# A new order of the four engines' queues in the expert feed-forward stages of a macaron block

## The reference

```
sim    = h @ Wq against the keys               # 4 heads, 2 x 64 keys
scores = top 8 of (top 8 of sx + top 8 of sy)  # pairs of keys = experts
w      = silu((h . down_embed) * softmax(scores))
experts = sum over chosen experts of w * up_embed
dense   = silu(h @ W_up.T) @ W_down.T          # 1024 hidden
x = x + 0.5 * (dense + experts)
```

## Time and profile before

| | |
|---|---|
| median of 3 runs | 3957.12 us (3955.64 to 3960.07) |
| profiled execution | 3957.12 us, span 3955.3 us |
| granted TensorE clock, mean | 0.973 |
| PE busy | 3690.7 us, 93% |
| DVE busy | 3255.2 us, 82% |
| ACT busy | 2747.0 us, 69% |
| POOL busy | 2457.3 us, 62% |

### The profile page before, as it was taken

One profiled execution on the slowest core, in us unless ns is written; L12 is line 12 of the kernel. 1 busy time (PEld: TensorE's weight loads), 2 busy tenths in 40 slices (PEclk: granted clock), 3 DMA queues, 4 the chain that ended last, 5 costly groups with the idle time before them and its releaser, 6 DMA issues. The chain is left out here.

```text
span 3955.3 us, 79090 instructions
## 1 busy us (share of the span) xinstructions
PE 3690.7 (93%) x27416; PEld 3206.7 (81%) x27416; DVE 3255.2 (82%) x7738; ACT 2747.0 (69%) x7878; POOL 2457.3 (62%) x2330
## 2 busy tenths in 40 slices
PE   6999999999779999999998699999999978999989
PEld 5888888888668888888887488888888867898878
DVE  7999999999668888888876799999999957756677
ACT  5677776777379999999996577777677737632166
POOL 6777787777355465555541678777787736511366
PEclk8999999999889999999998799999999998999999
DMA  4555555555500000000000456555555552421442
GB/s 106 114 121 120 116 118 114 116 118 115 113 26 13 18 18 23 13 23 13 23 7 12 111 114 123 117 118 116 114 118 118 115 108 88 128 97 59 129 147 91
DMA packets 190349, 343.11 MB, mean 87 GB/s; under 512 B 14816, under 2 KB 138112, under 8 KB 189952
## 3 DMA queue, kind: packets, MB, share of 16 engines
q0 software_dynamic: 55296, 201.35, 27.0%
q1 hardware_dynamic: 134656, 136.71, 10.8%
HBM read 80.06 MB, written 56.62 MB: 35 GB/s over the span
## 5 line engine op out<-in xcount | busy, mean ns | idle before, releaser
L302 POOL TENSOR_TENSOR f_grid<-f_ex 128x1024 f32<-128x1024 f32 x512 | 1088.8, 2168 | 10.5 <-DVE f_q L720 9.8
L1542 ACT ACTIVATE a_ex<-a_p_s,a_mneg 128x128 f32<-128x128 f32 x2048 | 730.1, 408 | 91.7 <-DVE a_mneg L1596 91.7
L711 DVE SCALAR_TENSOR_TENSOR f_p_u<-f_grid,f_te,f_p_dot 128x1024 f32<-128x1024 f32 x512 | 655.5, 1280 | 55.2 <-PE f_p_dot L106 54.4
L720 DVE SCALAR_TENSOR_TENSOR f_q<-f_p_u,f_rz,f_grid 128x1024 f32<-128x1024 f32 x512 | 655.6, 1280 | 4.8
L312 POOL DMA_DIRECT2D f_q<-f_q x384 | 364.6, 950 | 426.7 <-DMA f_q<-f_q 267.9
L1542 ACT ACTIVATION_READ_ACCUMULATOR a_ex<-a_p_s,a_mneg 128x1 f32 x2048 | 505.2, 247 | 0.0
L448 PE MATMUL f_p_y<-f_wdn,f_hs 128*128 128x256 f32 x2048 | 484.2, 385 | 0.7 <-DVE f_yt L736 0.5
L453 PE MATMUL f_p_y<-f_eup,f_wT 128*128 128x256 f32 x2048 | 472.9, 379 | 0.0
L448 PEld LDWEIGHTS f_p_y<-f_wdn,f_hs 128*128 128x128 f32 x2048 | 378.7, 192 | 48.5 <-issue 1.6
L453 PEld LDWEIGHTS f_p_y<-f_eup,f_wT 128*128 128x128 f32 x2048 | 379.8, 190 | 46.6
L1596 DVE TENSOR_REDUCE a_mneg<-a_p_s 128x4 f32<-128x512 f32 x512 | 335.6, 677 | 6.2 <-PE a_p_s L1396 6.2
(11 more groups left out here) (645 smaller groups left out, 11086.8 us busy)
## 6 DMA issues: line engine op xcount, KB each, us to landing
f_q<-f_q POOLq DMA_DIRECT2D x384, 512.0 KB, 4.7
x_f<-f_yt SPq DMA_DIRECT2D x64, 256.0 KB, 2.4
f_xt<-x SPq DMA_DIRECT2D x32, 256.0 KB, 5.9
a_xt<-x_f SPq DMA_DIRECT2D x16, 512.0 KB, 3.8
x_a<-a_yt SPq DMA_DIRECT2D x16, 512.0 KB, 3.0
f_xt<-x_a SPq DMA_DIRECT2D x32, 256.0 KB, 5.6
c_xt<-x_f SPq DMA_DIRECT2D x16, 512.0 KB, 4.7
x_c<-c_yt SPq DMA_DIRECT2D x16, 512.0 KB, 3.1
```

What stands on the lines that cost most here:

```text
L302: g_grid.mark(pool.tensor_tensor(grid[v][:, hd, :].rearrange("p (i j) -> p i j", i=XROWS), sx[:, hd, :].unsqueeze(2).to_broadcast([P, XROW ...
L711: d_mask.mark(dve.scalar_tensor_tensor(out=p_u[:], in0=grid[v][:, hd, :], scalar=te[:, v, hd, TOP - 1:TOP], in1=p_dot[:], op0=ALU.is_ge, o ...
L720: d_mul.mark(dve.scalar_tensor_tensor(out=q[v][:, hd, :], in0=p_u[:], scalar=rz[:, v, hd:hd + 1], in1=grid[v][:, hd, :], op0=ALU.mult, op1 ...
L1542: last = act.activation(ex[t.step % 2][:, i, n, :], p_s[i][:, n, :], ACT.Exp, bias=mneg[:, i, n:n + 1], accum_out=z[t.step % 2][:, i, n:n ...
```

## The change

On POOL, the first grid of the next turn goes ahead of the last accumulation of the turn before, and the last grid ahead of the accumulation summed(t, 1, 1). On PE, turn_w(t, 0, 0) moves from the end of a step to the start of the next, after dots(t + 1, 0), and the group turn_w(t, 0, 1) behind dense(t, 0, 1) and turn_h; experts(t - 1, 1, 1) moves from between hidden(t, 2) and hidden(t, 3) to before them. On ACT, turned(t, 0, 0) follows to the next step, and front(t, 1) and third(t, 1) move ahead of hidden(t, 2). On DVE, turned(t + 2) moves from after weigh(t, 0, 1) to right after weigh(t, 0, 0). No instruction is added or taken away.

```diff
--- before.py
+++ after.py
@@ -344,10 +344,12 @@
                 def step(t):
                     after = (t + 1).exists(last=count)
                     tails(t, 0)
+                    if after:
+                        scores(t + 1, 0, (0,))
                     if (t - 1).exists():
                         summed(t - 1, 1, 2)
                     if after:
-                        scores(t + 1, 0, (0, 1))
+                        scores(t + 1, 0, (1,))
                     summed(t, 0, 0)
                     if after:
                         pairs(t + 1, 0)
@@ -369,10 +371,8 @@
                         pairs(t + 1, 1)
                     clamps(t, 1)
                     if after:
-                        scores(t + 1, 1, (2,))
+                        scores(t + 1, 1, (2, 3))
                     summed(t, 1, 1)
-                    if after:
-                        scores(t + 1, 1, (3,))
                 turns(pool, count, unroll, step)
                 summed(end, 1, 2)
 
@@ -476,10 +476,12 @@
                 def step(t):
                     before, after, later = (t - 1).exists(), (t + 1).exists(last=count), (t + 2).exists(last=count)
                     if before:
-                        turn_w(t - 1, 0, 1)
+                        turn_w(t - 1, 0, 0)
                         dense(t - 1, 0, 1)
                     if later:
                         turn_h(t + 2)
+                    if before:
+                        turn_w(t - 1, 0, 1)
                     hidden(t, 0)
                     if before:
                         experts(t - 1, 0, 0)
@@ -497,17 +499,16 @@
                         dense(t - 1, 1, 0)
                         dense(t - 1, 1, 1)
                         experts(t - 1, 1, 0)
+                        experts(t - 1, 1, 1)
                     hidden(t, 2)
-                    if before:
-                        experts(t - 1, 1, 1)
                     hidden(t, 3)
                     dense(t, 0, 0)
-                    turn_w(t, 0, 0)
                     if after:
                         dots(t + 1, 0)
                 turns(pe, count, unroll, step)
+                turn_w(end, 0, 0)
+                dense(end, 0, 1)
                 turn_w(end, 0, 1)
-                dense(end, 0, 1)
                 for k in range(2):
                     experts(end, 0, k)
                 for k in range(2):
@@ -612,9 +613,11 @@
                 def step(t):
                     before, later = (t - 1).exists(), (t + 2).exists(last=count)
                     if before:
-                        turned(t - 1, 0, 1)
+                        turned(t - 1, 0, 0)
                     if later:
                         turn_h(t + 2)
+                    if before:
+                        turned(t - 1, 0, 1)
                     hidden(t, 0)
                     front(t, 0)
                     if later:
@@ -632,18 +635,17 @@
                         turned(t - 1, 1, 1)
                     if later:
                         exps(t + 2, 1)
+                    front(t, 1)
+                    third(t, 1)
                     hidden(t, 2)
-                    front(t, 1)
                     hidden(t, 3)
-                    third(t, 1)
-                    turned(t, 0, 0)
                     back(t, 1)
                     if (t + 3).exists(last=count):
                         normed(t + 3)
                 turns(act, count, unroll, step)
-                turned(end, 0, 1)
-                for k in range(2):
-                    turned(end, 1, k)
+                for v in range(V):
+                    for k in range(2):
+                        turned(end, v, k)
 
             @block.vector
             def _(dve):
@@ -773,14 +775,14 @@
                     for v in range(V):
                         mask(t, v, 0)
                         weigh(t, v, 0)
+                        if v == 0 and later:
+                            turned(t + 2)
                         if after:
                             maxes(t + 1, v, range(0, 3))
                         mask(t, v, 1)
                         if after:
                             maxes(t + 1, v, range(3, 5))
                         weigh(t, v, 1)
-                        if v == 0 and later:
-                            turned(t + 2)
                         if after:
                             maxes(t + 1, v, range(5, 8))
                         mask(t, v, 2)
```

## The result

The changed kernel takes 4210.79 us (median of three, 4209.57 to 4218.57) against 3957.12: 254 us slower, ratio 1.0645 (95% interval 1.0621 to 1.0669). I had said 4080, and at most 4160. The sign and the main mechanism were right, the size was not: two terms of the period were put at nothing, of about 1.0 and 1.6 us a turn.

The account below looks back on a forecast made before the run. PE (30.36 of 31.76 us busy) and DVE (29.66) nearly filled the turn. The new period 17.07 + 16.55 = 33.62 against 31.63, +1.99 us over 62 steps, gave +123 us: 4080 us, range 4032 to 4160.

Parts of the forecast that it names:

- ScalarE's order and PE's standstill at hidden(3): The Silu of p_hid queues behind front(t,1) and third(t,1), so PE stands still 3.2 us every turn before hidden(3).
- the terms 8.39 + 0.99 + 0.60 + 0.06: From mask(t,1,0) start: to weigh(t,1,2) end 8.39 us, third and handover 0.99, Silu of p_hid 0.60, on to PE 0.06.
- Transposes (0,0) move ... Cost nothing by itself: On PE, moving these transposes after dots(t+1,0) takes 0.36 us off the path before the next turn, at no cost.
- the 0.69 that I had for turned: On DVE, turned(t+2), moved right after weigh(t,0,0), newly waits 0.69 us for ScalarE's copy.
- the part T0 to M: DVE from mask(t,0,0) start (T0) to mask(t,1,0) start (M): forecast 17.07 us, 17.65 before.
- I take none for the forecast: No low-clock cost counted after PE's standstill; it would be 1.28 us a turn, 4159 us, if every one did it.
- Rival (a): PE's clock falls in most turns after its recurring 3 us standstill: 4110 to 4160 us, chance 0.15.
- the part M to T0: DVE from mask(t,1,0) start to the next turn's mask(t,0,0) start: forecast 16.55 us, 14.11 before.
- The DMA wait: PE's wait for the accumulating DMA, 84.7 us in 63 waits, goes away but for a few at the stages' ends.
- (b): DVE's new wait at turned is hidden, by an earlier ACT copy or later DVE: 4036 to 4051 us, chance 0.06.
- (c): PE's standstill is hidden and only its DMA wait goes: turn 30.36 us, 3878 us, faster, chance 0.06.
- (d): No change: gain and loss cancel, which needs a PE standstill of just 1.3 us; chance 0.03.

Follow-up runs that it names:

- Experiment 5: Kernel before with only ScalarE's new order front(t,1), third(t,1), hidden(t,2), hidden(t,3): 4106.48 us, ratio 1.0386.
- experiment 9: Changed kernel with the Silu of hidden(t,2) put between front(t,1) and third(t,1) on ScalarE: 3999.62 us, ratio 1.0117.
- experiment 2: Changed kernel with the transposes (0,0) put back at the end of a step, on PE and ScalarE: 4186.47 us, ratio 1.0593.
- experiment 7: Kernel before with only the transposes (0,0) moved behind dots(t+1,0), on PE and ScalarE: 3972.95 us, ratio 1.0045.
- experiment 3: Changed kernel with experts(t-1,1,1) back between hidden(t,2) and hidden(t,3) on PE: 4203.32 us, ratio 1.0635.
- experiment 4: Changed kernel with eight unread 512-column matmuls added on PE between hidden(t,2) and hidden(t,3): 4124.04 us, ratio 1.0432.
- run 62: Not a follow-up run: the whole run of the changed kernel, 4210.79 us; 62 is its steps from turn to turn, 31 in each of two stages.
- experiment 1: Changed kernel with ScalarE's old order put back (Silu of hidden(t,2), front(t,1), hidden(t,3), third(t,1)): 4017.35 us, ratio 1.0162.

## Why the prediction was right in sign and wrong in size

*ScalarE's order and PE's standstill at hidden(3): right.* The chain from weigh(t,1,2) over third, the Silu, hidden(3), dense and dots to mask is in the trace of after, step for step. From M to the start of hidden(3) it is 540.66 - 530.65 = 10.01 us, where the terms 8.39 + 0.99 + 0.60 + 0.06 give 10.04. PE's waits sum to 204 us where I said near 190, a turn's wait is 2.9 to 3.1 where I said 3.05. Experiment 5 shows that this edit alone makes most of the loss, experiment 9 that third alone is what holds the Silu up.

*"Transposes (0,0) move ... Cost nothing by itself": the first step that failed.* I asked who waits for p_wT, and not who overwrites what the transposes read. They read q of head 0, and weigh(t,0,0) writes it again; line 719 of the kernel before makes it wait for turn_w(t-1,0,1). That group now stands behind dots, the transposes (0,0), dense and turn_h. The wait is 1.82 us in the turn shown and comes 62 times, 111.4 us in all. It hides the 0.69 that I had for turned, so the part T0 to M was short by 1.0 us: 18.07 against 17.07. Experiments 2 and 7 show both waits where the steps of the new account have them.

*"I take none for the forecast": the clock.* This is the larger of the two steps. The term was put at 0 and measured 1.6 us a turn (experiments 3, 4 and 5), in 56 turns 90 us, of which experiment 4 shows 87. Rival (a) was right in mechanism and a little low in price, 1.28. In the changed kernel the low clock followed all 56 waits of the middle turns. I gave it 0.15 on two earlier waits of 3.1 and 3.2 us, one of which was followed by it, and said that few waits were so long. The trace of the kernel before had more to judge by among PE's waits for the accumulation in the two expert stages:

```profile
183.48 0.92 PE L436 MATMUL f_p_wT<-f_ident,f_q 128*128 128x128 f32 x4 [2.50 <-DMA f_q<-f_q]
...
657.66 0.66 PE L436 MATMUL f_p_wT<-f_ident,f_q 128*128 128x128 f32 x4 [2.91 <-DMA f_q<-f_q]
...
1006.07 0.90 PE L436 MATMUL f_p_wT<-f_ident,f_q 128*128 128x128 f32 x4 [2.75 <-DMA f_q<-f_q]
...
2517.92 0.66 PE L436 MATMUL f_p_wT<-f_ident,f_q 128*128 128x128 f32 x4 [2.95 <-DMA f_q<-f_q]
```

Behind each of these four the mean granted clock of the next 4 us is 0.57. With 3.13 (low clock) and 2.43 and 3.22 (full clock) that makes five of seven waits between 2.4 and 3.3 us, not one of two. Read so, a low clock in most turns was the likelier case, and with the 1.28 of the earlier trace rows the forecast would have been near 4160, still without the transposes. The Trainium skill's description of a wait that returns and is paid each time (TensorE: Matmul & The Clock Gate, section "HAM oscillation — how this bites in real kernels") agrees with this trace, where the low clock came back behind each of those 56 waits.

Together: 33.62 + 1.0 for the weigh that waits, + 1.6 for the clock, - 0.3 for the part M to T0 at full clock is 35.9, the period measured. VectorE's wait for p_dot, 4.0 to 4.4 us in place of the 2.9 forecast, holds the clock too: it is 2.66 in experiment 4. For the run 62 x (35.94 - 31.63) = 267 us. From the first T0 of a stage to its last it is 1108.8 and 1108.9 us, against 980.8 and 978.0 before: 259, less since PE's wait shrinks in the last three turns. The result has 254; the few us that are left lie outside these 62 steps and I did not resolve them. The range failed because its top held one missing term, the clock, and the sum missed another beside it.

*The DMA wait:* PE's wait for the accumulation fell by 50 us, not by all; the turns shown keep 0.3 to 0.9 us. I had said that it goes away but for the stages' ends. That gain is not in the time, since PE stands still for 3 us later in the same turn. GpSimd now waits for VectorE at the grids (499 us over the run, in 187 waits). The largest in a turn is that of the grid queued ahead, which waits for weigh(t,0,0) as foreseen: 6.4 to 6.7 us a turn, with weigh's own new wait in it.

*The rivals (b), (c), (d):* the wait of turned was hidden as in (b), but by a larger one. (c) and (d) needed a standstill under 1.3 us; it is 3.

*Not settled:* why moving turned alone gains 20 us, why moving experts(1,1) alone costs only 29, why hidden(3) and dense run 0.3 us shorter here than in the kernel before, and which of several equal waits is followed by the low clock.

## What to carry to other kernels

When an instruction is moved, follow three kinds of waiters: who needs its result, who needs its buffer, and who overwrites what it reads. The third has no data to point at and is found only among the waits in the code. In a loop where two engines are within a tenth of the period, a read that frees a single buffer must not stand behind work that hangs on a third engine; one Silu one place earlier in ScalarE's queue was worth 211 us here. And price a recurring standstill of TensorE of some 3 us twice, once for its length and once for the low clock behind it (1.6 us a turn here). For how likely that is, count every wait of such a length in the trace before, not only the two nearest.

## What the runs showed of the hardware

After waits of 2.6 to 3.5 us for the Silu, coming back each turn, PE's granted clock mostly fell to 0.50 for about 3 us of its next work: 56 of 56 times in the changed kernel, 49 of 56 in experiment 5, 50 of 54 in experiment 3, 49 of 54 in experiment 2. It stayed at 1.00 after four waits of 3.12 to 3.16 us in experiment 3, and once, in the kernel before, after 3.22 us. After waits of 2.2 us it did either (2.17 low, 2.18 not, in the changed kernel). After the waits of 0.7 to 1.6 us in experiments 1, 4 and 9 it never fell (the first of each stage, over 5 us, left aside). So in these runs the length of a wait alone does not say whether the clock falls. The fall doesn't always come with the first matmul: behind a wait of 3.14 us hidden(3) ran at 0.98 and dense, right after it, at 0.50. Each low stretch cost 1.6 us of the turn. Idle time filled with matmuls that nobody reads made the kernel 87 us faster.
